# Causal attention on one core: the scale of the scores moves from the exponential to the eviction of Q

## The reference

```python
hidden = layernorm(x)                                   # 2 x 1024 x 256
qkv = lora_linear(hidden, w_attn, b_attn, la_attn, lb_attn)
q, k, v = split and laid out by heads
def fake_quant(x, scale, zero_point):
    q = jnp.clip(round_ste(x / scale + zero_point), QMIN, QMAX)
    return (q - zero_point) * scale
k = fake_quant(k, kv_scale, kv_zero_point)
v = fake_quant(v, kv_scale, kv_zero_point)
scores = jnp.einsum('bhqd,bhkd->bhqk', q, k) / math.sqrt(HEAD_DIM)
scores = jnp.where(causal, scores, -jnp.inf)
attn = jax.nn.softmax(scores, axis=-1)
out = jnp.einsum('bhqk,bhkd->bhqd', attn, v)
```

## Time and profile before

| | |
|---|---|
| median of 3 runs | 2668.6 us (2663.5 to 2671.62) |
| span of the profiled execution | 2667.6 us, 39071 instructions |
| busy share of the span | PE 75%, DVE 61%, ACT 41%, POOL 32% |
| the attention stage | from 92.4 us (first product L753) to 429.8 (last L915) |
| its exponentials (L876) | 384, 206.7 us busy on ACT |

### The profile page before, as it was taken

How to read it: one execution, slowest core, us unless ns; L and a number is a source line. 1 busy time by engine, 2 the same in 40 slices (tenths; PEclk the granted TensorE clock), 3 DMA queues, 4 the chain that set the end, 5 groups by cost and what they waited for, 6 DMA issues and landing times. The chain is left out here.

```text
span 2667.6 us, 39071 instructions
## 1 busy us (share of the span) xinstructions
PE 2004.0 (75%) x14341; PEld 1036.0 (39%) x14401; DVE 1620.7 (61%) x2986; ACT 1080.7 (41%) x1890; POOL 840.8 (32%) x1016
## 2 busy tenths in 40 slices
PE   6688888888479987789999834887456593289991
PEld 3333334323232234233333312443232263268991
DVE  3767763486348864778888447994683405366442
ACT  3277774143113434477777622222210312144330
POOL 3122320243214441666465202322171000412225
PEclk9689997898679998799999976778678797589996
DMA  5100001000100002000000041000110200343113
GB/s 183 55 23 22 25 14 30 0 1 2 34 0 1 1 12 119 33 32 27 34 27 35 30 150 55 2 2 3 52 47 32 69 0 5 118 155 127 49 45 102
DMA packets 79900, 117.12 MB, mean 44 GB/s; under 512 B 17815, under 2 KB 57763, under 8 KB 78181
## 3 DMA queue, kind: packets, MB, share of 16 engines
q1 hardware_dynamic: 71125, 102.72, 11.3%
q0 software_dynamic: 3664, 9.32, 1.2%
q10 hardware_dynamic: 4928, 2.62, 0.4%
HBM read 80.23 MB, written 34.14 MB: 43 GB/s over the span
## 5 line engine op out<-in xcount | busy, mean ns | idle before, releaser
L1181 DVE TENSOR_REDUCE a_mx<-a_SM 128x2 f32<-128x1024 f32 x256 | 299.8, 1217 | 66.6 <-PE a_SM L1054 66.3
L1164 ACT ACTIVATE a_P<-a_ST 128x512 f32<-128x512 f32 x512 | 292.7, 598 | 106.1 <-PE a_ST L1080 105.0
L876 ACT ACTIVATE a_P<-a_ST,a_scale 128x512 f32<-128x512 f32 (+3 forms) x384 | 206.7, 589 | 86.8 <-PE a_ST L788 85.1
L891 DVE TENSOR_REDUCE a_mx<-a_SM 128x2 f32<-128x1024 f32 (+1 forms) x192 | 176.4, 952 | 68.4 <-PE a_SM L753 37.6
L1080 PE MATMUL a_ST<-a_Q,a_K 98*128 98x512 bf16 (+1 forms) x456 | 168.1, 392 | 28.2 <-DMA a_Q<-a_MS 15.3
L1099 PE MATMUL a_OP<-a_P,a_V 128*32 128x256 f32 (+1 forms) x1792 | 157.9, 424 | 10.1 <-ACT a_P L1164 6.5
L723 POOL TENSOR_SCALAR_AFFINE_SELECT a_P<-a_P 128x128 f32<-128x128 f32 (+1 forms) x256 | 77.7, 308 | 245.3 <-ACT a_P L876 244.1
L3193 POOL CAST work<-work 128x512 bf16<-128x512 f32 x92 | 74.0, 844 | 208.5 <-PE experts_py L3282 194.1
L788 PE MATMUL a_ST<-a_Q,a_K 50*128 50x512 bf16 (+3 forms) x384 | 119.2, 359 | 24.7 <-ACT a_P L876 24.3
L3362 DVE TENSOR_TENSOR experts_hl<-work 128x512 bf16<-128x512 f32 x92 | 83.8, 969 | 80.8 <-POOL work L3193 80.8
L3266 PE MATMUL experts_ph<-experts_x,experts_w1h 128*128 128x256 bf16 x736 | 127.1, 276 | 3.4 <-DVE experts_x L3356 1.7
(11 more groups left out here) (586 smaller groups left out, 4588.9 us busy)
## 6 DMA issues: line engine op xcount, KB each, us to landing
work<-L_ffn_W SPq DMA_DIRECT2D x16, 1024.0 KB, 6.0
conv_tab<-dft_tables SPq DMA_DIRECT2D x8, 1024.0 KB, 4.9
bias_hankel<-bias_rows SPq DMA_DIRECT2D x16, 448.0 KB, 5.9
a_K<-a_k_parts SPq DMA_DIRECT2D x96, 64.0 KB
a_Q<-a_q_parts SPq DMA_DIRECT2D x96, 64.0 KB
expert_rows<-zeros SPq DMA_DIRECT2D x1, 5888.0 KB, 22.9
experts_x<-expert_rows SPq DMA_DIRECT2D x23, 256.0 KB, 2.9
expert_results<-params SPq DMA_DIRECT2D x23, 256.0 KB, 2.2
```

The source lines that it names most:

```text
L876: act.activation(Pr[:, s % 2, u, j, c0:N], ST[:, u, c0:N], ACT.Exp, scale=kscale[:, 0:1]).then_inc(exp_done, 1)
L891: dve.tensor_reduce(mx[:, g % 2, qt, k0 // N, :], SM[:, c % 2, :, 0:kn], AX.X, ALU.max).then_inc(mx_read, 1)
L1164: act.activation(Pr[:, s % 2, u, j, :], ST[:, (4 * s + x) % 2, :], ACT.Exp, scale=scale).then_inc(exp_done, 1)
L1181: dve.tensor_reduce(mx[:, g % 2, qt, k0 // N, :], SM[:, c % 2, :, :], AX.X, ALU.max).then_inc(mx_read, 1)
```

## The change

The factor `kscale` is multiplied into Q when ACT evicts it, as the scale operand of that instruction; since the bias of Q has to be multiplied too, DVE first makes `bq` = bias times `kscale` (one instruction on 128x2), and ACT waits for it before its first eviction of Q. The eviction of K stays as it was. The 384 exponentials lose their scale operand, a tile of one column, and take the constant 1 instead. No instruction changes its place on any engine, and one is added, on DVE.

```diff
--- before.py
+++ after.py
@@ -330,7 +330,8 @@
         pm = st.ps("mm", [P, 6, N])
         mm, ev, evv, vlink, klink = st.sem("mm"), st.sem("ev"), st.sem("evv"), st.sem("vlink"), st.sem("klink")
         inv, stored, ones_done = st.sem("inv"), st.sem("stored"), st.sem("ones_done")
-        kint, qhi, qmid = st.sem("kint"), st.sem("qhi"), st.sem("qmid")
+        kint, qhi, qmid, scaled = st.sem("kint"), st.sem("qhi"), st.sem("qmid"), st.sem("scaled")
+        bq = st.sb("bq", [P, DC])
         qlo, qr1 = [st.sem(f"qlo{c}") for c in range(DC)], [st.sem(f"qr1{c}") for c in range(DC)]
         jobs = [(w, c, t) for c in range(DC) for w in (1, 0) for t in range(TN)]
         nv = TT // 2
@@ -384,7 +385,11 @@
                         m = (2 * c + 1 - w) * TN + t
                         dst = (QF, KF)[w][:, c, t * N:(t + 1) * N]
                         act.wait_ge(mm, m + 1)
-                        act.activation(dst, pm[:, m % 6, :], ACT.Identity, bias=bqk[:, w, c:c + 1]).then_inc(ev, 1)
+                        if w:
+                            act.activation(dst, pm[:, m % 6, :], ACT.Identity, bias=bqk[:, 1, c:c + 1]).then_inc(ev, 1)
+                            continue
+                        act.wait_ge(scaled, 1)
+                        act.activation(dst, pm[:, m % 6, :], ACT.Identity, bias=bq[:, c:c + 1], scale=kscale[:, 0:1]).then_inc(ev, 1)
 
                 def high(c):
                     act.wait_ge(ev, (2 * c + 2) * TN)
@@ -440,6 +445,7 @@
                 dve.reciprocal(qs[:, 2:3], qs[:, 0:1]).then_inc(inv, 1)
                 dve.tensor_scalar(kscale[:], qs[:, 0:1], scale, None, ALU.mult).then_inc(inv, 1)
                 dve.wait_ge(inv, 2)
+                dve.tensor_scalar(bq[:], bqk[:, 0, :], kscale[:, 0:1], None, ALU.mult).then_inc(scaled, 1)
                 whole(0)
                 whole(1)
                 dve.wait_ge(qhi, 2)
@@ -620,7 +626,7 @@
                 low(len(pairs) - 1)
 
 
-def causal_attention(nc, K, name, QP, KP, Qs, Ks, slots, ld, V, Y, kscale):
+def causal_attention(nc, K, name, QP, KP, Qs, Ks, slots, ld, V, Y):
 
     HP = NH // 2
     NG = B * HP
@@ -873,8 +879,7 @@
                         act.wait_ge(st_ready, 4 * s + x + 1)
                         if x == 0 and s >= 2:
                             act.wait_ge(pv_done, s - 1)
-                        act.activation(Pr[:, s % 2, u, j, c0:N], ST[:, u, c0:N], ACT.Exp,
-                                       scale=kscale[:, 0:1]).then_inc(exp_done, 1)
+                        act.activation(Pr[:, s % 2, u, j, c0:N], ST[:, u, c0:N], ACT.Exp).then_inc(exp_done, 1)
                         if x == 0 and event(turned_at, s):
                             turned(*event(turned_at, s))
                         if x == 1 and event(rows_at, s):
@@ -3485,7 +3490,7 @@
                       beside=lambda st: LoraWeights(st, K, Wt, la, lb, (w_loaded, 48)))
             quantized_projections(nc, K, "a0_qkv", Wt, QP, KP, V, (bqk, bv), quant, (b_loaded, 64), kscale, HD ** -0.5,
                                   (Qs, Ks, slots, ld))
-            causal_attention(nc, K, "a0", QP, KP, Qs, Ks, slots, ld, V, K.XN, kscale)
+            causal_attention(nc, K, "a0", QP, KP, Qs, Ks, slots, ld, V, K.XN)
         with ExitStack() as cross:
             W = [cross.enter_context(nc.sbuf_tensor(f"c0_W{x}", shape, F32)) for x, shape in
                  (("q", [P, DC, 1, 8 * WD]), ("k", [CW_P, CW_N, 1, 8 * WD]), ("v", [CW_P, CW_N, 1, 8 * WD]))]
```

## The result

| | before | after |
|---|---|---|
| median of four runs each | 2667.0 us (2663.5 to 2671.6) | 2641.9 us (2638.7 to 2644.7) |
| ratio, with its 95% interval | | 0.991 (0.9891 to 0.9929) |
| span of the profiled execution | 2667.6 us | 2640.0 us |
| L876, now L882 (exponentials): busy, mean | 206.7 us, 589 ns | 174.9 us, 500 ns |
| steady lap | 18.72 us | 17.80 us |

Six lines are added above, so before's L876, L788, L806, L856, L863, L891 and L911 are L882, L794, L812, L862, L869, L896 and L916 now, and L387 is L392 for Q.

A forecast was written before the change was run, and what follows sets the result against it. A ring of ACT exponentials and PE waits was taken to bound each lap; 14 x 1.01 + 2 x 0.5 = 15.1 us, less 0.1 for Q's last eviction, gave 15.0 saved: median 2653.6 us, range 2646 to 2664.

The forecast's parts named there:

- The ring: Chain of ACT and PE waits around one 18.72 us lap of this attention; shortens by 1.01 us and stays the longest.
- Rival 1: DVE's L911 and L915 behind the reductions become the limit; only 5 to 10 us saved, 2658.5 to 2663.5; chance 0.18.
- Rival 3: The operand isn't what makes L876 dearer, exponentials stay at 685 ns; 2668.7 us; chance 0.04.
- Rival 2: All PE idle time is due to ACT; up to 2.0 us a lap, 2637; middle case 1.3, 2648; chance 0.07.
- The duration: Each 512-column exponential without the operand falls from 685 to 598 ns, 0.087 us saved; the same for narrower ones.
- The pitch: Start to start from an exponential to the next ACT instruction shrinks by 0.12 to 0.13 us, taken as 0.11.
- the count of four and six: Per lap, four exponentials save their duration (4 x 0.087) and six their pitch (6 x 0.11): 1.01 us.
- The laps: 16 laps of the stage: 14 save 1.01 us, the two long ones at its start 0.5 each; 15.1 us.
- Rival 4: PE's clock stays at its lower level for further laps; gain lost beyond 3.2, 2677 from 5; 0.05 with other costly shifts.
- PE's idle time: PE idle 2.17 of 20 us, 2.0 a lap, so the 1.01 saved fits; PE then busy about 18.8.
- Q's evictions: Eight evictions at L387 gain a scale operand, 0.11 us each, to about 0.80; only the last costs, 0.1 us.
- The new DVE instruction: The added 128x2 instruction costs 0 to 0.13 us, hidden by 11 us before Q's first eviction.

The follow-up runs named there:

- e2: The changed kernel with a tile of ones as the exponentials' scale operand; 2664.9 us, ratio 0.9987 to the kernel before.
- e7: The kernel before with a column of zeros as bias operand too, so two operands in each exponential; 2719.1 us, ratio 1.0186.
- before_again: The kernel before, unaltered, profiled a second time; one run, 2667.2 us.
- before_third: The kernel before, unaltered, profiled a third time; one run, 2665.7 us.
- e1: The kernel before with the exponentials' scale as a constant number, Q evicted as before; 2646.5 us, ratio 0.9915.
- e3: The changed kernel with a tile of ones as the exponentials' scale operand from the fourth group of heads on; 2660.2 us, ratio 0.9967 to before.
- after_again: The changed kernel, unaltered, profiled again and timed beside the kernel before; 2645.4 us, ratio 0.9908.
- e5: The kernel before with 64 more matmuls of 512 columns at the end of the projections, never read; 2674.8 us, ratio 1.0023.

## Why the prediction was partly right and wrong in size

**The ring, its members, and that it stays the longest: right.** The steady lap lost 0.92 us where 1.01 were forecast, member by member the same waits. Rival 1 is out: DVE's reciprocal still waited for PE and the laps are 17.80, not 18.1 to 18.4. Rival 3 is out by e2. Rival 2 asked for steady laps shorter by 1.3 or more; there are none.

**The duration: right.** 0.089 against 0.087 us.

**The pitch: over-sized by 0.02.** Two exponentials in a row went from 1.28 us to 1.11 (136.45), 0.17 for one duration and one pitch, so 0.085 for the pitch. An exponential with the cast behind it went from 0.58 between starts to 0.49 (133.47 to 133.96). I had taken 0.11, from the 1.06 us of two in a row in the other attention; this row isn't matched in this stage, and why it is shorter there stays open. With the measured 0.089 and 0.085 the count of four and six gives 0.87, 0.05 short of the lap's 0.92. The Trainium skill, "ScalarE: Activation LUTs", section "What ACT_TABLE_LOAD costs", was the better source: about 93 ns for each pointer operand and one overlap for all neighbours, which gives an estimate of 10 x 0.093 = 0.93 a lap. The trace agrees with 0.92; the 1.01 of e7 for the next operand is above it. This term was too large by 1.3 us over 14 laps, in the other direction than the miss.

**The laps: the step that failed.** "I give the two long laps half" took the 23.43 us of the earlier trace rows for a trait of the stage's start. They are laps in which PE runs at its lower clock for 14 us or more. The same program put them elsewhere the next time (before_again, before_third), and how many there are went with what the exponentials cost. Over three profiles of each kernel, the stretch from the first to the last exponential took 311.9 us before and 292.0 after, 19.9 less:
- the ring, 15 x 0.915 = 13.7;
- the excess, 7.5 before and 2.1 after: 5.3;
- the last lap, in which the maxima are over and the clock is low in both kernels (0.57 and 0.56 granted in the stretch of the last products): 0.8.

Another 0.4 lies before the first exponential. The timed difference over all runs is 23.1 us (means of 52 runs of before and 11 of after), so some 3 us are not located. What follows the last exponential took 2242 to 2247 us in the three profiles of before and 2240 to 2254 in those of after, with no change in it. The first pair of profiles happened to show before at its highest excess and after at its lowest, which is why their spans differ by 27.6. That the first result was so large was in part luck; the 23 us over all runs are not.

**Rival 4 had the mechanism and looked one way only.** It named the clock, priced a lap at the lower level at 4.7 us from the earlier trace rows, and noted that "shorter waits leave PE fewer gaps". It then spent this argument against a loss. The same argument is one for a gain, and it was given "a lap or so" at 0.04. With the earlier trace rows it could have been sized: with both long laps gone, 2 x 4.7 = 9.4 us, and each of them then saves the whole 1.0 instead of half, another 1.0. That is a case of 2653.6 - 10.4 = 2643, and the range should have reached to it.

**PE's idle time is not headroom.** I wrote that a lap's 2.0 us of idle PE left room for the 1.01, and that PE would be busy 18.8 of 20 us. It is busy 17.88, with 180 matmuls instead of 167. Over ten whole steady laps of each (178.44 to 365.62 before, 171.58 to 349.60 after) PE's busy time a lap went from 16.5 to 15.7 us and its idle time from 2.17 to 2.12. So most of the gain came out of what the profile calls busy. Both have 1520 matmuls there with the same recorded durations, which add up to 53.3 us a lap: the records overlap, and a wait shorter than a record vanishes under the one before it. What changed is the mean time from the start of a score's product (L788) to the next matmul's, 158 ns before and 130 after, which is 0.67 of the 0.92 us. The room wasn't where I had measured it, and the bound of rival 2 (2.0 a lap) was drawn from a number that doesn't bound.

**Q's evictions: right**, 0.78 for a forecast of 0.80, and e1 shows no cost of that half. **The new DVE instruction: wrong, and covered.** I bounded it at 0.13 us by its neighbour. The timeline of after:

```profile
33.59 2.65 POOL L415 MEMSET a_K<- 32x3072 bf16 x1 [13.22 <-POOLq L185]
...
33.71 0.14 DVE L446 TENSOR_SCALAR a_scale<-a_quant 128x1 f32<-128x1 f32 x1
33.88 2.39 DVE L448 TENSOR_SCALAR a_qkv_bq<-a_bqk,a_scale 128x2 f32<-128x2 f32 x1
```

It took 2.39 us, eighteen times the bound. The 11 us of cover before Q's first eviction hid it all the same.

## What to carry to other kernels

Count an ACTIVATE's per-partition operand at 0.09 us in its duration and nearly as much in the pitch to the next (0.065 to 0.09 in these exponentials), and count it only for those on the ring; a scale that can be folded into a step with idle time around it costs nothing there. When laps of one loop differ in one profile, look at the granted clock first: if they are laps at the lower level, their number is not fixed. It changed here together with the cost of the exponentials, and in e7 this came to 37 us beside 15 from the ring. So price one such lap from the trace and set a case for it on both sides.

## What the runs showed of the hardware that I had not expected

- **The clock of this matmul loop, fed by ScalarE, fell back more often the dearer the ScalarE step was.** With PE busy 88 to 89% of the undisturbed laps by the profile in all kinds, it fell 0 times in six profiles at 596 ns an exponential, once or twice in five at 685, and ten times in the one at 770. It isn't a rule for each lap: e3 has 12 laps at 685 ns without a fall. With one operand such a fall lengthened a lap of 18.72 us to 22.9 to 26.0. What exactly makes it fall isn't settled: PE's single waits for ScalarE are of up to 0.94 us before and its idle time in an undisturbed lap is 2.12, 2.17 and 2.23 us with none, one and two operands, so it hardly grew, and no run here varied the waits with the ScalarE time held. The Trainium skill, "TensorE: Matmul & The Clock Gate", section "A second HAM failure mode: psum-queue depth-cycling", describes short idle times between groups of matmuls that make the clock swing between its levels. The ten falls of e7 look like that; that the idle times are their cause was only argued.
- **Two executions of one program differ in their clock by several us.** After's first rise came at 115.3 or at 134.3 us, for an excess of 0.1 or 6.1 us (after, after_again), and before's fall at 120, 151 or 158 us. Late rises were seen only without the operand (3 of 6 profiles, 0 of 7 with it); whether that is chance stays open.
- **A clock that was up just before isn't kept.** In e5 it was up (1.00) from 78 to 92 us and fell at 95.4, in a stretch from 92 to 108 in which PE was busy 8.51 of 16 us.
- **A small DVE instruction can take 2.39 us beside a GpSimd memset.** L448 ran from 33.88 to 36.27, and the memset from 33.59 to 36.24. In all eight profiles with L448 it took 2.39 us and ended 0.03 us after that memset. The Trainium skill, "SBUF — State Buffer", section "SBUF: two separate sides", says that the two engines share a pair of ports, that a DVE instruction takes the pair only in a two-port mode or when it has two inputs in SBUF (then only against a GpSimd instruction that reads SBUF), and that whichever engine starts first holds the pair for its whole instruction while the other blocks. The ends fit that. But L446, with one column instead of two, ran beside the same memset in 0.14 us. The profile doesn't show an instruction's mode, and no run here took the memset away, so it stays an explanation that was only argued.
